# Decoder layer on one core: the dt chain of a step begun a step earlier, its parts set at other places, and its softplus correction made by VectorE

## The reference, cut to what matters

```python
zxbcdt = x @ in_proj_w.T                  # split into z, xv, Bm, Cm, dt_in
dt = softplus(dt_in @ dt_proj_w.T + dt_proj_b)
dA = exp(dt[..., None] * -exp(A_log))
dtx = (dt * x_full).reshape(b, l, GC, D_INNER // GC)
dBx = (dtx[..., :, None] * Bg[..., None, :]).reshape(b, l, D_INNER, D_STATE)
def step(h, inp):
    dA_i, dBx_i, C_i = inp
    h = dA_i * h + dBx_i                  # 16 states per channel, 1024 channels
    y = einsum('bgn,bgcn->bgc', C_i, h.reshape(b, GC, D_INNER // GC, D_STATE))
    return (h, y.reshape(b, D_INNER))
y = (scan(step) + D_skip * x_full) * silu(z)
```

## Time and profile before

| what | value |
|---|---|
| median of 3 runs | 2798.21 us |
| the profiled execution | 2799.06 us, its span 2797.3 us |
| busy in the span: PE, DVE, ACT, POOL | 2618.7, 2082.0, 1191.1, 1285.8 us |
| `scan` (L1401) | 512 times, 622.5 us |
| `read_out` (L1233) | 512 times, 662.9 us |
| mean granted clock of PE | 0.96 |

### The profile page before, as it was taken

How to read it: one execution, slowest core, us unless ns; L and a number is a source line. 1 busy time by engine, 2 the same in 40 slices (tenths; PEclk the granted TensorE clock), 3 DMA queues, 4 the chain that set the end, 5 groups by cost and what they waited for, 6 DMA issues and landing times.

```text
span 2797.3 us, 32656 instructions
## 1 busy us (share of the span) xinstructions
PE 2618.7 (94%) x11152; PEld 1877.7 (67%) x11160; DVE 2082.0 (74%) x2656; ACT 1191.1 (43%) x1786; POOL 1285.8 (46%) x868
## 2 busy tenths in 40 slices
PE   7888888898889879999999999999999999999999
PEld 4443444454345337888888778788878788888887
DVE  5999899999999976543376677777877865555553
ACT  5655555555555635422254543343333422222221
POOL 4899899899999961210001023123222422222220
PEclk9999899899899879999999999999999999999999
DMA  7754655555465437121111112112111121111111
GB/s 248 220 165 129 180 150 139 166 158 148 125 182 160 132 113 266 54 76 53 62 51 61 40 44 69 46 46 68 46 39 46 45 53 46 51 48 50 49 46 68
DMA packets 152311, 275.37 MB, mean 98 GB/s; under 512 B 27344, under 2 KB 27856, under 8 KB 151632
## 3 DMA queue, kind: packets, MB, share of 16 engines
q1 hardware_dynamic: 152144, 273.27, 32.7%
HBM read 178.01 MB, written 61.34 MB: 86 GB/s over the span
## 4 chain that ended last, share of the span: by engine, by line
PE 66%; DVE 9%; issue 8%; POOL 8%; ACT 4%; DMA 3%; SPq 1%; POOLq 0%; DVEq 0%; ACTq 0%
PE ps L1757 19%; PE ps L1759 19%; PE ps L1758 19%; DVE state L1401 4%; POOL read L1233 4%; PE ps L1806 3%; PE ps L1822 3%; ACT ps L896 1%; DMA vpack<-vl 1%; DMA b_d<-ev 1%; PE ps L1966 1%; POOL dt_t L1197 1%; POOL sp_rest L1182 1%; PE ps L1940 1%; DMA uraw<-y_d 1%
## 5 line engine op out<-in xcount | busy, mean ns | idle before, releaser
L1233 POOL TENSOR_TENSOR read<-state,c_t 128x512 f32<-128x512 f32 x512 | 662.9, 1316 | 74.4 <-DVE state L1401 35.8
L1401 DVE TENSOR_TENSOR_SCAN state<-ps,drive 128x512 f32<-128x512 f32 x512 | 622.5, 1216 | 4.2 <-ACT ps L896 1.7
L1295 POOL TENSOR_TENSOR wdeq<-packed,scales 128x1024 f32<-128x1024 f16 x96 | 256.2, 2668 | 800.7 <-DVE packed L1530 800.7
L1757 PE MATMUL ps<-xh,ghi 128*128 128x512 f32 x1536 | 607.3, 395 | 0.0
L1759 PE MATMUL ps<-xh,glo 128*128 128x512 f32 x1536 | 598.0, 389 | 0.0
L1758 PE MATMUL ps<-xl,ghi 128*128 128x512 f32 x1536 | 597.8, 389 | 0.0
L896 ACT ACTIVATE ps<-ps,a_exp 128x512 f32<-128x512 f32 x512 | 337.2, 661 | 385.4 <-PE ps L1806 383.9
L1392 DVE TENSOR_TENSOR drive<-ps,b_t 128x512 f32<-128x512 f32 x512 | 344.2, 672 | 53.6 <-PE ps L1806 49.5
L1697 DVE TENSOR_TENSOR act_o<-act_o,ps 128x512 f32<-128x512 f32 x192 | 131.8, 686 | 284.6 <-PE ps L1759 283.2
L1153 ACT ACTIVATE ahi<-act_o 128x512 fp32r<-128x512 f32 x192 | 121.6, 633 | 520.6 <-DVE act_o L1697 520.6
L1757 PEld LDWEIGHTS ps<-xh,ghi 128*128 128x128 f32 x1536 | 288.4, 188 | 62.6 <-issue 3.1
(11 more groups left out here) (197 smaller groups left out, 3842.0 us busy)
## 6 DMA issues: line engine op xcount, KB each, us to landing
whi<-w_d SPq DMA_DIRECT2D x63, 256.0 KB, 4.9
wlo<-w_d SPq DMA_DIRECT2D x63, 256.0 KB, 5.5
b_d<-ev SPq DMA_DIRECT2D x32, 256.0 KB
dpack<-dh SPq DMA_DIRECT2D x64, 128.0 KB, 4.4
dpack<-dl SPq DMA_DIRECT2D x64, 128.0 KB, 2.3
b_t<-b_d SPq DMA_DIRECT2D x32, 256.0 KB, 5.4
vpack<-vh SPq DMA_DIRECT2D x64, 128.0 KB, 2.3
vpack<-vl SPq DMA_DIRECT2D x64, 128.0 KB, 2.4
```

Of the source, the lines that this page charges most:

```text
L1233: pool.tensor_tensor(read[:, n % RRING, :], state[:, n % SRING, :], c_t[:, g % 2, :], ALU.mult).then_inc(read_ready, 1)
L1295: pool.tensor_tensor(wdeq[:, :].rearrange("p (h n) -> p h n", h=2), codes, scale, ALU.mult).then_inc(deq, 1)
L1401: dve.tensor_tensor_scan(state[:, n % SRING, :], ps[:, decay_bank(n), :], drive[:, n % DRING, :], 0.0, ALU.mult, ALU.add)\
L1757: pe.matmul(out_, w_h, x_h, start=(start and k == 0), stop=False)
```

## The change

A step q is called late where q is a multiple of 8 or q <= 4. For those the places stay as they were. For the 24 others (early):

- `dt_project(q)` goes from c = 11 of step q - 2 to c = 0 of the same step, ahead of the projection and the gather there.
- ACT makes their softplus at c = 3 to 7 of step q - 2 (was 12 to 15), and `dt_high`, `v_high` at c = 0 and 2 of step q - 1 (were 6 and 8).
- POOL makes `soft_sum`, `soft_dt`, `dt_x` at c = 10, 12, 14 of step q - 2 (were c = 1, 2, 3 of step q - 1), and `dt_low`, `v_low` at c = 1 and 4 of step q - 1 (were 7 and 9).
- SP issues the loads of x, `dpack` and `vpack` earlier in the step, ahead of the first spill.

For all 32, `soft_rest` is made by DVE: at c = 8, behind the scan, for early ones, at c = 15 for late ones, and ahead of the stage for q = 0. The banks of jobs change so that `dt_project` has bank 6 from q = 4 on.

```diff
+        def late(q):
+            return q % CT == 0 or q <= 4
+
         def dt_bank(q):
-
-            if q < 4:
-                return 7
+            return 7 if q < 4 else 6
+
+        def job_bank(job):
+            return 5 + job % 2 if job < 12 else 5 + job % IN_TILES % 3 % 2
+
+        def job_ahead(job):
+
+            m = job - 1
+            while m >= 0 and job_bank(m) != job_bank(job):
+                m -= 1
+            return m
...
-            return max([0] + [q + 1 for q in range(4, g + 2) if dt_bank(q) == 5 + job % 2])
+            if job < 12 or job_bank(job) == 5 or g < 3:
+                return 0
+            return g + 2 if late(g + 2) else g + 3
...
-                    sp.wait_ge(y_ready, q - 2)
+                    sp.wait_ge(gathered, 4 * (q - 3) + 1)
...
+                if jobs and late(g + 1):
                     spill(first)
                 if 0 <= g + 1 < STEPS:
                     load_c(g + 1)
+                if g + 2 < STEPS and not late(g + 2):
+                    load_x(g + 2)
+                if g + 1 < STEPS and not late(g + 1):
+                    load_pack_dt(g + 1)
+                    load_pack_v(g + 1)
+                if jobs and not late(g + 1):
+                    spill(first)
                 if g >= 1:
                     store_y(g - 1)
                 if jobs:
                     weights_after(first + 1)
-                if 0 <= g + 1 < STEPS:
+                if g + 1 < STEPS and late(g + 1):
                     load_pack_dt(g + 1)
                     load_pack_v(g + 1)
                 if jobs:
                     spill(first + 1)
-                if g + 2 < STEPS:
+                if g + 2 < STEPS and late(g + 2):
                     load_x(g + 2)
                 if jobs:
                     weights_after(first + 2)
...
-                        if c == 6:
+                        if c == (6 if late(g + 1) else 0):
                             dt_high(g + 1)
-                        if c == 8:
+                        if c == (8 if late(g + 1) else 2):
                             v_high(g + 1)
-                    if nb < B:
+                    if nb < B and late(g + 2):
...
+                            soft_log(g + 2)
+                    elif nb < B:
+                        if c == 3:
+                            soft_abs(g + 2)
+                        if c == 4:
+                            soft_pos(g + 2)
+                        if c == 5:
+                            soft_exp(g + 2)
+                        if c == 6:
+                            soft_one(g + 2)
+                        if c == 7:
...
-            soft_rest(0)
...
-                    if g + 1 < STEPS:
-                        if c == 0:
-                            soft_rest(g + 1)
+                    if g + 1 < STEPS and late(g + 1):
...
+                    elif g + 1 < STEPS:
+                        if c == 1:
+                            dt_low(g + 1)
+                        if c == 4:
+                            v_low(g + 1)
+                    if g + 2 < STEPS and not late(g + 2):
+                        if c == 10:
+                            soft_sum(g + 2)
+                        if c == 12:
+                            soft_dt(g + 2)
+                        if c == 14:
+                            dt_x(g + 2)
...
+            def soft_rest(q):
+                dve.wait_ge(sp_one_ready, 2 * q + 2)
+                if q:
+                    dve.wait_ge(sp_sum_ready, q)
+                dve.tensor_tensor(sp_rest[:, :], sp_abs[:, :], sp_exp[:, :], ALU.add)\
+                   .then_inc(sp_rest_ready, 1)
...
+            soft_rest(0)
...
+                    if g == 0 and c == 0:
+                        soft_rest(1)
+                    if nb < B and c == (15 if late(g + 2) else 8):
+                        soft_rest(g + 2)
...
+                    if job_ahead(job) >= 0:
+                        if job_ahead(job) % IN_TILES == 0:
+                            pe.wait_ge(dtlo_ready, job_ahead(job) // IN_TILES + 1)
                         else:
-                            pe.wait_ge(job_taken, taken_count(job - 2))
...
+                    if nb < B and not late(g + 2) and c == 0:
+                        dt_project(g + 2)
                     if jobs and (c < 12 or g < 2):
                         project(first + c // 4, c % 4)
-                    if nb < B and c == (10 if g < 2 else 11):
+                    if nb < B and late(g + 2) and c == (10 if g < 2 else 11):
```

More of the change, by code:

```diff
@@ L374, in last_in_bank, with job_ahead_of_dt @@
             return m
+        def late(q):
+            return q % CT == 0 or q <= 4
         def dt_bank(q):
-            if q < 4:
-                return 7
-            nb, k, jobs = step_jobs(q - 2)
[L381 to L387, removed]
+            return 7 if q < 4 else 6
[6 more added lines that the diff above has]
+            return m
+        def job_ahead_of_dt(q):
+            nb, k, jobs = step_jobs(q - 2)
+            job = first_job(q - 2) + 2 * late(q) if jobs else IN_TILES * (nb + 1)
+            return job_ahead(job) if job_bank(job) == 6 else max(
+                j for j in range(job) if job_bank(j) == 6)
         def dt_ahead(job):
@@ L819, in take @@
                 act.wait_ge(job_done, job + 1)
-                bank = ps[:, 5 + job % 2, :]
+                bank = ps[:, job_bank(job), :]
                 if tile == 0:
@@ L1176, in normalise @@
                 pool.tensor_tensor(hat(b)[:, f, :], xlr[b][:, f, :], r1, ALU.mult).then_inc(ln_hat, 1)
[L1178 to L1183, removed]
             def soft_sum(q):
@@ L1381, in dt_split @@
                 dve.wait_ge(dthi_ready, nb + 1)
-                dve.tensor_tensor(dtlo[:, :], ps[:, 5 + (IN_TILES * nb) % 2, :],
+                dve.tensor_tensor(dtlo[:, :], ps[:, job_bank(IN_TILES * nb), :],
                                   dthi[:, :].bitcast(F32), ALU.subtract).then_inc(dtlo_ready, 1)
+            def soft_rest(q):
[4 more added lines that the diff above has]
+                   .then_inc(sp_rest_ready, 1)
             def make_drive(g, c):
@@ L1771, in project @@
                         pe.wait_ge(w_loaded[s], 32 * ((job - IN_TILES) // 3 + 1))
-                    if job >= 2:
-                        if (job - 2) % IN_TILES == 0:
-                            pe.wait_ge(dtlo_ready, nb + 1)
+                    if job_ahead(job) >= 0:
+                        if job_ahead(job) % IN_TILES == 0:
+                            pe.wait_ge(dtlo_ready, job_ahead(job) // IN_TILES + 1)
                         else:
-                            pe.wait_ge(job_taken, taken_count(job - 2))
+                            pe.wait_ge(job_taken, taken_count(job_ahead(job)))
                     if dt_ahead(job):
@@ L1780, in project @@
                     pe.wait_ge(ln_lo, FT * nb + f + 1)
-                mm = three_pass(ps[:, 5 + job % 2, :], [(whi[s][:, f, :], wlo[s][:, f, :],
+                mm = three_pass(ps[:, job_bank(job), :], [(whi[s][:, f, :], wlo[s][:, f, :],
                                                         xh[nb][:, f, :], xl[nb][:, f, :])],
@@ L1794, in dt_project @@
                 if q >= 4:
-                    job = last_job(dt_bank(q), q)
+                    job = job_ahead_of_dt(q)
                     if job % IN_TILES == 0:
```

## The result

The changed kernel takes 2852.95 us, the median of 4 runs (2851.23 to 2855.60), beside 2796.85 us of the kernel before on the same chip (4 runs, 2793.29 to 2801.01). The ratio is 1.0201, with a 95% interval of 1.0183 to 1.0219: 56 us slower. The forecast of 2833 had the sign right and was 20 us short; the time lies above its range, which ended at 2850.

The account below looks back on a forecast made before the run. VectorE was taken to bound the scan stage, with TensorE making it late at a few places. 13.3 + 24.4 - 3.7 + 0.6 = +34.6 us on 2799.06 gave 2833.7, 2833 for a median; range 2800 to 2850.

Parts of the forecast that it names:

- (e): Waits added by the new order: 0 in the scan stage, +0.6 us before it, where `soft_rest(0)` holds up the first centring.
- (a): `soft_rest` on VectorE, the bound: mostly 0.7 us each, some swallowed by waits; +13.3 us, from +11 to +30.
- (b): `dt_project` at c = 0 adds three matmuls to TensorE's chain at the step boundary: +24.4 us, from 0 to +34.
- (c): Earlier dt chain: TensorE's `vpack` waits nearly all go, few reach VectorE; -3.7 us, at most -8.
- (d): GpSimd loses 31 operations of 1.25 us in the stage, but is not waited for: 0.
- Rival 1: Without `vpack` stops TensorE's clock stays at 2.4 GHz at the boundary and its waits go: -7.9 us, 2790, chance 0.12.
- Rival 2: GpSimd lags at c = 8, so each `soft_rest` costs the upper 1.57 us: +17 more, 2850, chance 0.13.
- Rivals 3 and 4: 3: boundary hides most of `dt_project`, 6 us not 24, 2815, chance 0.17; 4: GpSimd paces the stage, 2782, chance 0.04.

Follow-up runs that it names:

- (3): Changed kernel with a second `sp_pos` buffer for odd q: 2835.45 us, ratio 1.0128 to the kernel before, 20 us under the changed kernel.
- (5): Changed kernel with `soft_rest` back on GpSimd, at the sub-steps where VectorE had it: 2835.57 us, ratio 1.0130 to the kernel before.
- 2: Changed kernel with `dt_project` of the early steps at c = 1 instead of c = 0: 2837.92 us, ratio 1.0134 to the kernel before.
- (4): Changed kernel with one more matmul ahead of each spread of dt at c = 12 to 15: 2820.94 us, ratio 1.0076 to the kernel before.
- experiment 1: Changed kernel with every step treated as late, `soft_rest` kept on VectorE: 2808.24 us, ratio 1.0028 to the kernel before.

## Why the prediction was wrong in size and right in sign

**The step that failed is (e):** "The job with bank 6 (c = 4) waits for `soft_pos`, made by ACT at c = 4. ACT needs a spread, a decay and `soft_pos`, about 1.8 us from the end of scan 1, and TensorE comes there at about 2.2: 0." This counts ACT's own work and leaves out what ACT waits for: the single `sp_pos` is free only after `soft_dt` of the q before. Among early ones that is long done. At the four seams it is done at c = 2 of GpSimd's list, behind ACT's c = 4. Priced 0, it cost 16.9 us of waits, and 20 us undone (3). Each of the two orders was looked at by itself, not the passage from one to the other.

**(a), +13.3, was mis-sized:** `sp_rest` took 24.0 us of VectorE; undone it gave 20 (5). The single price held for most: 26 of 32 are 0.66 to 0.69 long and take 0.58, under the 0.7 taken. One thing that failed is the count. 19 of 31 were charged, and the 12 others, 12 x 0.58 = 7.0, were to be swallowed by waits. In steps 5, 13, 21 and 29 that is borne out: their waits at c = 10 fell from 4.9 to 1.0 (in the ledger among the other waits). In steps 7, 15 and 23 the wait behind `sp_rest` was one that the change removed, and the new one stands at c = 6, ahead of it. The other thing is five long ones, 1.30, 2.97, 1.53, 1.51 and 1.54 in steps 3, 5, 7, 15 and 23, 5.5 us above 0.66 together. Four of the five stand at the seams, where GpSimd makes `dl` of the late q at c = 7, right ahead of the early one's `sp_rest`. In step 7, GpSimd and VectorE:

```profile
315.43 1.30 POOL L1234 TENSOR_TENSOR dl<-dt_t,dh 128x512 fp32r<-128x512 f32 x1
316.68 1.74 POOL L1257 TENSOR_TENSOR read<-state,c_t 128x512 f32<-128x512 f32 x1
```

```profile
315.74 1.53 DVE L1422 TENSOR_TENSOR sp_rest<-sp_abs,sp_exp 128x512 f32<-128x512 f32 x1
```

The count of GpSimd's parts in (a) took c = 1 and 4, which holds among early ones only: the passage again. By the ledger (a) is short by 10.7. Another 6.0 us, the growth of VectorE's other operations that read SBUF twice, has no term in the sum; most of it comes with the chain's new places (5).

**(b), +24.4, was right in its sum, and that is in part luck:** 23.3 in the ledger, 24.0 in 2. The nine boundaries that had waited 1.33 gained 5.1 us where 12.6 were reckoned, and only four of them wait about the 2.7 that follows from it (2.54 to 2.61). The seven with 0.50 to 1.00 gained 8.0 (7.0 reckoned), and the eight others 10.2 (4.8 reckoned).

**(c), -3.7,** looks about right beside the -4.9 of the other waits, but only 2.0 of it, the wait at the end of step 4, is what (c) named; 3.9 are the waits at c = 10 that (a) has, and step 30's 1.20 is replaced by one of 1.67. TensorE's waits for `vpack` went as foreseen, from 27.4 us in 21 to 2.9 in 3. **(d), 0, was right:** no wait of VectorE is on a read-out, before or after. But the spills leave SP earlier too, and 12.5 us of waits for weights went: a gain that the prediction had not. It covered most of the failed step, and without it the time would have been further off.

**The miss of the sum,** 55.5 - 34.6 = 20.9, is then: (e) +16.9, the weights -12.5, (a) +10.7, the other operations that read SBUF twice +6.0, (b) -1.1, the other waits beyond (c) -1.2, scans and drives -2.4, the spread of the second stage +4.1, the start +0.3, in all 20.8.

**Rival 1 (the clock, 0.12)** named as cause that TensorE stands still for `vpack` before the boundary. The stops went and the clock stayed low, 0.88 in the stage. More work in c = 12 to 15 keeps it up (4). The rival reckoned 42.5 us between its own time and the forecast, for all 24 boundaries turned; with 19 of the 24 gathers at full speed, 4 gave 35. The Trainium skill (TensorE: Matmul & The Clock Gate, HAM oscillation — how this bites in real kernels) puts such a fall in a loop down to a wait for a DMA; here the waits went and the fall stayed.

**Rival 2 (the port, 0.13),** at 2850 the nearest to the time, is not the mechanism: it had `sp_rest` at 1.57 everywhere, 17 us more, and only five are long, with 5.5 us. **Rivals 3 and 4** did not happen: the boundaries wait more, and the bound is VectorE.

## What to carry to other kernels

Where a chain of several engines is moved ahead for some steps only, go through each passage from a step in the old order to one in the new, and for each single buffer ask when its last reader is done there: a wait for the engine named may be that engine's wait for a third. An operation added to the engine that sets the pace costs its full length unless the wait that is to swallow it outlives the change. And where an engine waits on TensorE at a low granted clock, try one more matmul in the thin stretch ahead, before taking work out of it. The gain is limited by what the engine would wait for next: it was 35 us in the changed kernel and 3 in the one before.

## What the runs showed of the hardware

- More work made TensorE faster. With three matmuls instead of two in the sub-steps 12 to 15, the granted clock over the boundary into step 17 is 1.00 instead of 0.50, the gather there 1.06 us instead of 1.94, and the kernel 35 us faster.
- 128x512 with two inputs in SBUF on VectorE is 0.66 us when GpSimd is idle at its start. Begun beside an operation of GpSimd it ends some 0.55 us behind that one's end (above, 315.74 + 1.53 = 317.27 beside 315.43 + 1.30 = 316.73), and GpSimd's next is the longer (1.74 instead of 1.27). The Trainium skill (SBUF — State Buffer, SBUF: two separate sides) has VectorE and GpSimd lock each other out for a whole instruction; these lengths agree.
- Sometimes VectorE does not come in at the first end. The 2.97 of step 5 lies beside the last two of four reads in a row and ends 0.55 behind the second:

```profile
245.75 4.99 POOL L1257 TENSOR_TENSOR read<-state,c_t 128x512 f32<-128x512 f32 x4
```

```profile
248.32 2.97 DVE L1422 TENSOR_TENSOR sp_rest<-sp_abs,sp_exp 128x512 f32<-128x512 f32 x1
```

The 5.03 and the 5.92 in experiment 1 lie beside four operations of GpSimd each. What lets GpSimd go on there, and not elsewhere, was not tried.
